# Cross-attention and mixture-of-experts kernel: new hand-written orders for all engines, no operation changed

## The chip, the cores and the metric

One core of one Trainium2 chip runs the kernel. The metric is device time in microseconds (us), from launch to the end. The profile comes from one such execution; its span is the time from the first to the last instruction on the core.

## What is computed

One transformer block on x of 4 x 256 x 256 (batch, position, width) in float32: a cross-attention with 16 heads of width 16 against a context of the same size, then a feed-forward part in which each position uses 2 of 8 experts. Cut to what matters:

```python
def attn(query, kv):                       # query = layernorm(x)
    Q, K, V = query @ Wq.T + bq, kv @ Wk.T + bk, kv @ Wv.T + bv
    a = softmax(einsum('bhsd,bhtd->bhst', Q, K) * 0.25)
    return einsum('bhst,bhtd->bhsd', a, V) @ Wo.T + bo
def ffn(x):                                # x = layernorm(x)
    scores = softmax(x @ G); w = scores kept for the 2 best experts, else 0
    out  = (silu(x @ gate) * (x @ up) * w) @ down
    return out + ((x @ lora_A) * w) @ lora_B
x = x + attn(layernorm(x), ctx)
x = x + ffn(layernorm(x))
```

## The kernel before, in words

Each of the four batches b is one tile of 256 positions. The whole program is cut into named stages, and every engine works through its own list of stages, written out by hand in `ORDERS`: "name:batch" or "name:batch.step", and for TensorE "@bank" with the PSUM bank that it writes (max and attn take that bank and the next). An engine runs its stages strictly in that order. Stages on different engines are tied by semaphores, so a stage whose input is late holds up all that is listed behind it on its engine. A TensorE stage also waits until the stage that last wrote its bank has been read out. SyncE issues nearly all transfers, also in its listed order.

The stages, in the order of the data, with the engine and the lines of the profile:

- st1, rs1, n1: layer norm of x. VectorE takes the moments (st1, L644 to L647), GpSimd makes 1/sqrt with a power (rs1, L431 to L437; shift at L437), ScalarE normalises (n1, L506; for batch 0 VectorE, L671). xT transposes it on TensorE (L857), xTE copies it out.
- k, v, q: the projections on TensorE (all products are at L813). khi, kw, qhi, qw (ScalarE, L525) and klo, qlo (VectorE L682 for batch 0, GpSimd L428) split k and q into two parts. vE (L532) copies v.
- kfill, qfill: memsets of the stacked tiles (GpSimd L393, VectorE L657, ScalarE L485); `ones` (L398) and `earlier` (L401, L402) are other constants on GpSimd. edge: two memsets of one column each on VectorE.
- ks0, ks1, qs0, qs1: SyncE copies the parts into the stacked tiles (L337, L344, L352, L359). Each ks and qs stage first waits for the fill of its tile. Batch 3 uses batch 0's tiles again. SyncE also issues wd, a weight of the last product (L302, L303).
- max (L886): scores, two heads at a time; mx (VectorE, L715): their row maxima. mrow (TensorE, L892) transposes the maxima once all eight mx of a batch are done, mrE (ScalarE, L538) copies them, ms (SyncE, L363) sends them into the stacked q.
- attn (L901): the scores again with the maximum taken off; e (ScalarE, L544): exponential; u (L911): times v. uT, rd (VectorE, L719, L725), um (GpSimd, L442), un (VectorE, L730): division by the sum. o: output product, after ah (ScalarE, L604) and al (VectorE, L778). x2 (VectorE, L734) adds it to x; xo (GpSimd, L448) has added the bias.
- st2, rs2, x2T (L933), x2hi, x2w, x2lo: the second layer norm's moments and transposes. low: gate logits and LoRA part, lowE copies it; r1, r2, ex, r3: weights of the experts. glu: gate and up products, in two steps; th (ScalarE, L582) and h (VectorE, L773, L775) their activation; wh (L318) and wl (L310) weigh them.
- hT, lT (L960, L965): transposes; hThi, lThi (ScalarE), hTlo (VectorE, L789) and lTlo (L793) split them; down: the last product, in two steps for batch 3; res (L802) adds, out stores.
- Weights: ws, wsl, wfc (L702), wlc, mean (L871), mlow take the mean out of the feed-forward weight; bw (VectorE, L688 to L692) and bias (L867), bp prepare the output bias. wkh, wkl, wvh, wvl, wfh, wfl, woh, wol, wdh, wdl split weights.

bw is a tensor_scalar and two additions. The wait at a stacked copy reads

```python
                if name == "qs0":
                    if b < NSTACK:
                        wait(sp, "qfill", b)
                    ...
                    wait(sp, "qhi", b)
                    for g in (0, 2):
                        sp.dma_start(part_rows(qstack[b], g), parts_of(q_hi[:, b % 2])).then_inc(q_stacked[b], 16)
```

Of the kernel before, what the change touches and what calls it, by code (L numbers as in the profile page):

```python
# [49 lines left out]

ORDERS = {
    "tensor": """
        k:0@6 xT:0@4 v:0@5 q:0@0 k:1@4 bias@5 xT:1@3 mean@0 v:1@2 max:0.4@0 max:0.3@6 xT:2@5 q:1@3 max:0.2@6
        max:0.0@4 max:0.1@0 v:2@2 k:2@3 max:0.5@0 max:0.7@6 max:0.6@4 q:2@2 max:1.0@0 max:1.1@6 xT:3@3 mrow:0@4
        k:3@5 max:1.2@2 max:1.3@6 q:3@4 max:1.4@2 attn:0.0@6 max:1.5@0 attn:0.1@2 max:1.6@6 attn:0.2@4 max:1.7@0
        attn:0.3@2 max:2.0@6 u:0.0@5 mrow:1@4 attn:0.4@0 max:2.1@2 attn:0.5@6 u:0.1@5 attn:0.6@0 max:2.2@2
        attn:0.7@6 u:0.2@5 attn:1.0@0 max:2.3@2 attn:1.1@6 u:0.3@5 attn:1.2@0 max:2.4@2 attn:1.3@6 u:1.0@5
        max:2.6@0 max:2.5@2 attn:1.4@6 o:0@4 attn:1.5@2 max:2.7@0 attn:1.6@6 u:1.1@5 max:3.1@2 max:3.0@0
        mrow:2@7 x2T:0@4 v:3@5 max:3.3@6 max:3.2@2 attn:1.7@0 mlow@4 u:1.2@5 attn:2.0@6 max:3.4@0 attn:2.1@2
        u:1.3@5 attn:2.3@0 attn:2.2@6 max:3.5@2 low:0@4 attn:2.5@0 attn:2.4@2 max:3.6@6 u:2.0@5 u:2.1@5  # L60
        attn:2.6@0 attn:2.7@2 max:3.7@6 glu:0.1@4 mrow:3@0 glu:0.0@7 o:1@6 attn:3.1@0 attn:3.3@2 attn:3.0@4
        u:2.2@7 u:2.3@7 attn:3.2@0 attn:3.4@4 attn:3.5@2 u:3.0@7 u:3.1@7 x2T:1@6 attn:3.6@4 attn:3.7@2 lT:0@1
# [6 lines left out]
        chi:3 qhi:1 qw:1 wfh n1:3 vE:2 khi:2 kw:2 qhi:2 xTE:3 mrE:0 qw:2 khi:3 kw:3 qhi:3 e:0.0 qw:3 e:0.1-3
        mrE:1 e:0.4-7 e:1.0-6 mrE:2 x2hi:0 x2w:0 vE:3 e:1.7 wdh e:2.0-1 e:2.3 e:2.2 woh e:2.5 e:2.4 lowE:0  # L70
        ah:1.1 e:2.6 ah:1.0 mrE:3 th:0.1 e:2.7 th:0.0 ex:0 ah:2.0 e:3.1 e:3.0 e:3.3 e:3.2 e:3.5 e:3.4 ah:2.1
        x2hi:1 x2w:1 e:3.6 lThi:0 e:3.7 ah:3.0 lowE:1 x2hi:2 hThi:0 ex:1 x2w:2 ah:3.1 th:1.0-1 lowE:2 ex:2
        x2hi:3 x2w:3 th:2.1 th:2.0 lowE:3 hThi:1 lThi:1 ex:3 th:3.1 th:3.0 hThi:2 lThi:2 lThi:3 hThi:3
    """,
    "vector": """
        warm edge kfill:2 kfill:0 st1:0 n1:0 st1:2 st1:1 klo:0 ws bw wsl qlo:0 st1:3 wfc mx:0.3-4 mx:0.2 mx:0.1
        mx:0.0 mx:0.5 mx:0.7 mx:0.6 mx:1.1 mx:1.0 mx:1.2-7 mx:2.0-1 uT:0.0 rd:0.0 mx:2.2 un:0.0 mx:2.3 uT:0.1
        rd:0.1 mx:2.4 un:0.1 mx:2.5-6 x2:0 mx:2.7 uT:1.0 mx:3.0-1 mx:3.3 mx:3.2 rd:1.0 mx:3.4 wlc uT:1.1 mx:3.5
        rd:1.1 st2:0 mx:3.6 un:1.1 un:1.0 uT:2.0 mx:3.7 al:1.0 rd:2.0 al:1.1 r1:0 un:2.0 h:0.1 h:0.0 r2:0 al:2.0
        x2:1 r3:0 uT:2.1 rd:2.1 st2:1 un:2.1 uT:3.0 al:2.1 rd:3.0 un:3.0 lTlo:0 x2:2 st2:2 r2:1 al:3.0 uT:3.1  # L80
# [944 lines left out]
```

## Time and profile before

| | us |
|---|---|
| median of 3 runs (109.81 to 111.5) | 110.0 |
| the profiled execution | 110.28 |
| its span | 108.5 |
| TensorE busy (matmuls) | 102.2 |
| VectorE busy | 92.0 |
| ScalarE busy | 76.7 |
| GpSimd busy | 55.4 |

Busy times add up what instructions of one engine take; the rest of the span the engine waits. Matmuls are pipelined and their ends are modelled, so a busy TensorE need not be at its peak. The granted TensorE clock is 1.0 of full speed over the whole span. A row of the timeline reads: start, length, engine, line, operation, what is written from what, number of instructions; in brackets the idle time ahead of it and who ended it.

### The profile page before, as it was taken

To read this page: it belongs to the slowest core of one execution; us is meant where nothing else is said; L and a number is where in the kernel's file an instruction comes from. 1 tells how busy PE (TensorE), PEld (TensorE's weight loads), DVE (VectorE), ACT (ScalarE), POOL (GpSimd) and SP (SyncE) were. 2 spreads that over 40 slices of the span, in tenths; PEclk is the share of its full clock that TensorE was granted. 3 is DMA by queue.
4 is the path that set the end of the run, shared out by engine and by line. 5 is a ranking of instruction groups with operands and counts; after the bars stand their busy time and mean duration, and the time that the engine had idled before them with its cause. 6 is when DMAs were issued, how large, how long until landed. Compare 5 with 4: busy or idle time off the path is not lost.

```text
span 108.5 us, 2396 instructions
## 1 busy us (share of the span) xinstructions
PE 102.2 (94%) x910; PEld 80.7 (74%) x910; DVE 92.0 (85%) x196; ACT 76.7 (71%) x140; POOL 55.4 (51%) x86
## 2 busy tenths in 40 slices
...
DMA packets 8469, 11.76 MB, mean 108 GB/s; under 512 B 713, under 2 KB 5002, under 8 KB 8458
## 3 DMA queue, kind: packets, MB, share of 16 engines
...
## 4 chain that ended last, share of the span: by engine, by line
PE 77%; DVE 6%; ACT 6%; POOL 6%; issue 2%; POOLq 0%
PE unit L813 40%; PE unit L911 12%; PE unit L901 9%; PE unit L886 8%; ACT probs L544 3%; DVE kstack L657 3%; PE unit L933 2%; POOL rstd L436 2%; PE unit L857 2%; PE unit L960 2%; POOL vaug L398 1%; DVE rowmax L715 1%; PE unit L892 1%; ACT xn L506 1%; PE unit L965 1%
## 5 line engine op out<-in xcount | busy, mean ns | idle before, releaser
L715 DVE TENSOR_REDUCE rowmax<-unit 128x4 f32<-128x1024 f32 x32 | 37.6, 1217 | 4.4 <-PE unit L886 4.3
L544 ACT ACTIVATE probs<-unit 128x1024 f32<-128x1024 f32 x32 | 31.2, 1027 | 2.7 <-PE unit L901 2.4
L911 PE MATMUL unit<-probs,vaug 128*32 128x256 f32 x256 | 16.3, 384 | 0.0
L901 PE MATMUL unit<-qstack,kstack 64*128 64x256 f32 x128 | 13.6, 310 | 1.1 <-DVE rowmax L715 0.7
L442 POOL TENSOR_TENSOR un<-uT,rden 128x256 f32<-128x256 f32 x8 | 5.0, 630 | 18.8 <-DVE rden L725 18.8
L901 PEld LDWEIGHTS unit<-qstack,kstack 64*128 64x128 f32 x128 | 9.1, 185 | 6.0 <-ACT probs L544 2.2
L886 PE MATMUL unit<-kstack,qstack 63*128 63x256 f32 x128 | 12.4, 296 | 0.6 <-ACT probs L544 0.6
L886 PEld LDWEIGHTS unit<-kstack,qstack 63*128 63x128 f32 x128 | 9.1, 185 | 3.5 <-issue 1.4
L911 PEld LDWEIGHTS unit<-probs,vaug 128*32 128x32 f32 x256 | 7.1, 109 | 5.1 <-ACT probs L544 0.2
L813 PE MATMUL unit<-xT,wq 128*128 128x256 f32 x32 | 7.8, 386 | 0.0
L813 PEld LDWEIGHTS unit<-xT,wq 128*128 128x128 f32 x32 | 5.8, 190 | 0.9
L719 DVE STREAM_TRANSPOSE uT<-unit 128x512 f32<-128x512 f32 x8 | 5.7, 710 | 0.8 <-PE unit L911 0.7
L463 POOL TENSOR_TENSOR x2T_lo<-x2T,x2T_hi 128x512 fp32r<-128x512 f32 x2 | 2.6, 1293 | 7.1 <-ACT x2T L563 7.1
L644 DVE BATCH_NORM_STATS2 stats<-xs 128x6 f32<-128x256 f32 x16 | 5.8, 403 | 0.0
L818 PE MATMUL unit<-warm 128*128 128x128 f32 x20 | 4.6, 429 | 1.1 <-DVE warm L655 1.1
L448 POOL TENSOR_TENSOR xs<-xs,bo_sb 128x256 f32<-128x256 f32 x8 | 5.6, 726 | 0.0
L525 ACT ACTIVATE q_hi<-unit,wq 128x256 fp32r<-128x256 f32 x8 | 3.3, 468 | 2.9 <-PE unit L813 2.9
L818 PEld LDWEIGHTS unit<-warm 128*128 128x128 f32 x20 | 4.3, 331 | 1.1 <-DVE warm L655 1.1
L428 POOL TENSOR_TENSOR q_lo<-q_whole,q_hi 128x512 fp32r<-128x512 f32 x3 | 3.9, 1290 | 2.1 <-ACT q_whole L525 2.1
L813 PE MATMUL unit<-wf,x2T 128*128 128x136 f32 x32 | 4.5, 283 | 0.0
L813 PEld LDWEIGHTS unit<-wf,x2T 128*128 128x128 f32 x32 | 4.1, 189 | 0.4 <-ACT x2T L563 0.2
L813 PE MATMUL unit<-cT,wk 128*128 128x256 f32 x16 | 4.3, 416 | 0.0
...
## 6 DMA issues: line engine op xcount, KB each, us to landing
kstack<-k_hi SPq DMA_DIRECT2D x8, 256.0 KB, 3.0
qstack<-q_hi SPq DMA_DIRECT2D x8, 256.0 KB, 2.6
xs<-x SPq DMA_DIRECT2D x4, 256.0 KB, 5.5
kstack<-k_lo SPq DMA_DIRECT2D x4, 256.0 KB, 3.3
qstack<-q_lo SPq DMA_DIRECT2D x4, 256.0 KB, 2.8
cT<-ctxT SPq DMA_DIRECT2D x3, 256.0 KB, 3.1
out<-xs SPq DMA_DIRECT2D x3, 256.0 KB, 2.5
...
```

The costliest lines, as they stand in the source:

```text
L428: pool.tensor_tensor(lo[:, b % 2], whole[:], hi[:, b % 2].bitcast(F32), ALU.subtract).then_inc(done[name], 1)
L442: pool.tensor_tensor(un[:, i].rearrange("p n h d -> p h n d"), uT[:, i, :, :, 0:HD], rden[:, i].unsqueeze(3).to_broadcast([P, 2, BLK, HD]) ...
L448: ins = pool.tensor_tensor(xs[:, b, t], xs[:, b, t], bo_sb[:], ALU.add)
L544: act.activation(probs[:, n % NPAIR], unit[BANK["attn", b, i] // 2][:], ACT.Exp, scale=SCALE)\
L644: ins = dve.bn_stats(stats[:, w, b, t], src[:, t])
L715: dve.tensor_reduce(rowmax[:, b % 2, :, :, i].rearrange("p t j -> p j t"), unit[BANK["max", b, i] // 2][:], AX.X, ALU.max).then_inc(done[" ...
L719: dve.transpose(uT[:, i].rearrange("p h n c -> p (h n c)"), work[BANK["u", b, 2 * i]].rearrange("p h s -> p (h s)")).then_inc(done["uT"], 1)
L813: ins = pe.matmul(dst, left(i, k), right(j, k), start=(n == 0), stop=(n == len(steps) - 1))
L818: pe.matmul(unit[3][:, 1, 0, 0:P], warm[:], warm[:], start=True, stop=True)
L886: ins = pe.matmul(pair[:, j, t], qstack[b][rows, i, t * P:(t + 1) * P], kstack[b][rows, i], start=True, stop=True)
L901: ins = pe.matmul(pair[:, j, t], kstack[b][rows, i, t * P:(t + 1) * P], qstack[b][rows, i], start=True, stop=True)
L911: ins = pe.matmul(dst[QUAD * j:QUAD * (j + 1), i % 2], vaug[:, b % NVALUE, t, 4 * i + j], probs[:, n % NPAIR, j % 2, t], start=(t == 0), s ...
```

## The change

All five lists of `ORDERS` are new; nothing else. Every stage stands in the lists as before and on the same engine, and every operation is as before; the waits follow from the lists. Two lines of the diff:

```diff
-        qfill:0 ident rs1:0 earlier ones rs1:2 rs1:1 rs1:3 wvl klo:1 clo:2 wkl qlo:1 clo:3 qfill:2 xo:2 klo:2
...
+        ident qfill:2 rs1:0 ones rs1:1 qfill:0 rs1:2 wvl klo:1 rs1:3 clo:2 wkl qlo:1 clo:3 xo:0 klo:2 qlo:2 xo:3
```

At the start of GpSimd's list, behind the ones of vaug and a first round of statistics (L431 to L437, which is batch 2 before and batch 1 now):

```order
 L436 TENSOR_TENSOR rstd<-vare,mhalf 128x2
 L437 TENSOR_TENSOR shift<-minus_mean,rstd 128x2
-L431 TENSOR_SCALAR vare<-mv 128x2
-L435 TENSOR_SCALAR minus_mean<-mv 128x2
-L436 TENSOR_TENSOR rstd<-vare,mhalf 128x2
-L437 TENSOR_TENSOR shift<-minus_mean,rstd 128x2
+L393 MEMSET qstack0 128x2048
 L431 TENSOR_SCALAR vare<-mv 128x2
 L435 TENSOR_SCALAR minus_mean<-mv 128x2
```

A round of statistics between the first and the next has gone back (batch 3's now comes behind wvl and klo:1), batch 1's and batch 2's have changed places, and the memset of qstack0, which stood first on GpSimd, has come in behind batch 1's. ScalarE's n1:1 and n1:2 and SyncE's x:1 and x:2 have changed places in the same way, wf is loaded ahead of x:2 and wo, and on TensorE bias has gone behind xT:1 and mean.

On TensorE, around the maxima of batch 0 (L892, mrow:0), before, from xT:3 (L857) and k:3 (the six pairs on cT and wk) to q:3 (L813 on xT and wq); kstack1 is batch 1:

```order
L886 MATMUL unit3<-kstack1,qstack1 128x256 x4
L857 MATMUL unit1<-ident,xn 128x128 x4
L892 MATMUL unit2<-ident,rowmax 16x128 x2
L813 MATMUL unit2<-cT_hi,wk_hi 128x256 x2
...
L886 MATMUL unit1<-kstack1,qstack1 128x256 x4
L886 MATMUL unit3<-kstack1,qstack1 128x256 x4
L813 MATMUL unit2<-xT,wq 128x256 x4
```

and now:

```order
L857 MATMUL unit1<-ident,xn 128x128 x4
L813 MATMUL unit2<-cT_hi,wk_hi 128x256 x2
...
L886 MATMUL unit1<-kstack1,qstack1 128x256 x4
L886 MATMUL unit3<-kstack1,qstack1 128x256 x4
L892 MATMUL unit2<-ident,rowmax 16x128 x2
L813 MATMUL unit0<-xT,wq 128x256 x4
```

mrow:0 has moved behind k:3 and two score pairs, directly ahead of q:3. On ScalarE mrE:0 now follows khi:3 and kw:3, and qw:3 comes ahead of e:0.0 instead of behind it; on SyncE ms:0 follows ks1:2, qs0:2 and ks0:2.

At the end of VectorE's list, before, from the last h (L773, L775) to the first res (L802):

```order
L773 SCALAR_TENSOR_TENSOR hid<-hid,unit 128x256
L775 TENSOR_TENSOR hid<-hid,unit 128x256
L318 TENSOR_TENSOR hid<-hid,weight_hid 128x256
L310 TENSOR_TENSOR low<-low,weight_low 128x128 x2
L793 TENSOR_TENSOR q_lo<-unit,q_hi 128x256
L318 TENSOR_TENSOR hid<-hid,weight_hid 128x256
L789 TENSOR_TENSOR k_lo<-unit,k_hi 128x512
L802 TENSOR_TENSOR xs<-unit,xs 128x512
```

and now:

```order
L773 SCALAR_TENSOR_TENSOR hid<-hid,unit 128x256
L775 TENSOR_TENSOR hid<-hid,unit 128x256
L310 TENSOR_TENSOR low<-low,weight_low 128x128 x2
L318 TENSOR_TENSOR hid<-hid,weight_hid 128x256 x2
L789 TENSOR_TENSOR k_lo<-unit,k_hi 128x512
L793 TENSOR_TENSOR q_lo<-unit,q_hi 128x256
L802 TENSOR_TENSOR xs<-unit,xs 128x512 x2
```

lTlo:2 (L793) and hTlo:2 (L789) have gone behind wl:3 (L310) and both wh:3 (L318). Further up, hTlo:0 has gone from ahead of un:3.1 to behind al:3.1, h:1.1 and r1:2, and lTlo:0 from ahead of x2:2 to ahead of rd:3.1. On TensorE lT:3 now writes bank 4, as hT:2 does, and comes behind hT:3.

For batch 3, SyncE's list was "qs1:3 ks1:3 qs0:3 ks0:3" and is "ks1:3 ks0:3 qs0:3 qs1:3 wd"; GpSimd's was "um:0.0 qlo:3 klo:3" and is "qlo:3 um:0.0 earlier klo:3". Where the feed-forward part of batch 0 begins, x2T:0 has gone behind v:3 on TensorE, and u:2.2 shares bank 5 with glu:0.1 now, where it was bank 7 with glu:0.0; VectorE's "h:0.1 h:0.0 r2:0" is "r2:0 h:0.0-1", and ScalarE's "e:2.7 th:0.0" is "wdh th:0.0".

## Rows read from the trace of the kernel before

**Rows 1.** Stretch, length, busy us of TensorE, weight loads, VectorE, ScalarE, GpSimd; clock.

```profile
84.67:101.20 16.53, 16.53 (x115) 15.04 (x114) 15.64 (x56) 8.12 (x25) 7.66 (x15) 1.00 0.01 1
```

**Rows 2.** Timeline of the start, 0 to 19 us.

```profile
0.78 1.81 POOL L393 MEMSET qstack<- 128x2048 f32 x1 [0.29 <-POOLq L1016]
...
10.17 0.72 POOL L436 TENSOR_TENSOR rstd<-vare,mhalf 128x2 f32<-128x2 f32 x1
...
11.44 0.35 DVE L688 TENSOR_SCALAR hid<-wo 128x256 f32<-128x256 f32 x1
...
11.61 1.09 ACT L506 ACTIVATE xn<-xs,shift,rstd 128x256 f32<-128x256 f32 x2 [0.29 <-POOL shift L437]
...
12.34 0.41 DVE L692 TENSOR_TENSOR hid<-hid,bo_row 1x256 f32<-1x256 f32 x1
...
12.35 1.19 POOL L436 TENSOR_TENSOR rstd<-vare,mhalf 128x2 f32<-128x2 f32 x1
...
13.99 0.59 PE L867 MATMUL unit<-hid,warm 128*128 128x256 f32 x2
...
14.99 0.66 PE L857 MATMUL unit<-ident,xn 128*128 128x128 f32 x4 [0.41 <-ACT xn L506]
...
18.16 0.74 PE L886 MATMUL unit<-kstack,qstack 63*128 63x256 f32 x8
```

**Rows 3.** Timeline of SyncE's issues, over the whole span.

```profile
13.50 1.18 SPq L352 DMA_DIRECT2D qstack<-q_hi  x2
...
14.72 0.61 SPq L359 DMA_DIRECT2D qstack<-q_lo  x1
...
30.15 0.64 SPq L363 DMA_DIRECT2D qstack<-mT  x1
...
46.23 2.71 SPq L352 DMA_DIRECT2D qstack<-q_hi  x2
...
48.98 1.26 SPq L337 DMA_DIRECT2D kstack<-k_hi  x2
```

**Rows 4.** Issues in narrow stretches (14.6 to 14.8, 49.55 to 49.7): size, us to landing.

```profile
qstack<-q_lo SPq DMA_DIRECT2D x1, 256.0 KB, 2.6
...
kstack<-k_hi SPq DMA_DIRECT2D x2, 256.0 KB, 3.1
```

**Rows 5.** Timeline around the first exponentials, 26 to 39 us.

```profile
31.75 0.84 ACT L525 ACTIVATE k_whole<-unit,wk 128x256 f32<-128x256 f32 x2
...
33.87 0.50 PE L901 MATMUL unit<-qstack,kstack 64*128 64x256 f32 x4
...
36.05 2.86 ACT L544 ACTIVATE probs<-unit 128x1024 f32<-128x1024 f32 x3
...
38.05 1.07 PE L911 MATMUL unit<-probs,vaug 128*32 128x256 f32 x16
```

**Rows 6.** Timeline of the passage to batch 3 and to the feed-forward part.

```profile
52.88 0.74 PE L886 MATMUL unit<-kstack,qstack 63*128 63x256 f32 x8 [0.63 <-ACT probs L544]
...
67.88 0.36 ACT L538 CAST mT<-unit 16x256 fp32r<-16x256 f32 x1 [0.95 <-PE unit L892]
...
70.36 0.42 DVE L775 TENSOR_TENSOR hid<-hid,unit 128x256 f32<-128x256 f32 x1
...
70.57 0.97 PE L901 MATMUL unit<-qstack,kstack 64*128 64x256 f32 x12
...
71.48 1.93 PE L911 MATMUL unit<-probs,vaug 128*32 128x256 f32 x32
```

**Rows 7.** Timeline of VectorE and TensorE towards the end.

```profile
83.94 0.69 DVE L789 TENSOR_TENSOR k_lo<-unit,k_hi 128x512 fp32r<-128x512 f32 x1
...
84.67 0.45 DVE L730 STREAM_TRANSPOSE attnT<-un 128x256 f32<-128x256 f32 x1
...
100.52 0.68 DVE L789 TENSOR_TENSOR k_lo<-unit,k_hi 128x512 fp32r<-128x512 f32 x1
...
101.35 0.47 PE L813 MATMUL unit<-cT_hi,k_hi 128*128 128x256 f32 x2
```

More of the change, by code:

```diff
@@ L52 @@
     "tensor": """
[L53 to L62, printed above, removed]
@@ L63 @@
-        o:2@7 low:1@0 u:3.2@5 u:3.3@5 x2T:2@6 hT:0@0 glu:1.0@2 glu:1.1@1 low:2@0 o:3@3 lT:1@7 glu:2.1@6 x2T:3@4
-        glu:2.0@3 low:3@5 hT:1@1 glu:3.0@2 lT:2@4 glu:3.1@0 down:0@5 hT:2@0 down:1@1 lT:3@6 hT:3@4 down:2@7
-        down:3.1@6 down:3.0@3
+        k:0@3 xT:0@1 v:0@4 q:0@5 k:1@0 xT:1@4 mean@1 bias@6 v:1@3 max:0.4@6 max:0.3@0 xT:2@5 q:1@3 max:0.2@6
+        max:0.0@4 max:0.1@0 v:2@2 k:2@3 max:0.5@0 max:0.7@6 max:0.6@4 q:2@2 max:1.0@0 max:1.1@6 xT:3@3 k:3@4
+        max:1.3@2 max:1.2@6 mrow:0@5 q:3@1 max:1.4@2 max:1.5@4 attn:0.0@6 attn:0.1@0 max:1.6@2 attn:0.2@4
@@ new lines @@
+        max:2.0@6 max:1.7@0 attn:0.3@2 u:0.0@4 mrow:1@5 attn:0.4@0 max:2.1@2 attn:0.5@6 u:0.1@4 attn:0.6@0
+        max:2.2@2 attn:0.7@6 u:0.2@5 attn:1.0@0 max:2.3@2 attn:1.1@6 u:0.3@5 attn:1.2@0 max:2.4@2 attn:1.3@6
+        u:1.0@5 max:2.6@0 max:2.5@2 attn:1.4@6 o:0@4 attn:1.5@2 max:2.7@0 attn:1.6@6 u:1.1@5 max:3.1@2 max:3.0@0
+        max:3.3@6 mrow:2@4 v:3@5 x2T:0@4 attn:1.7@0 max:3.2@2 u:1.2@5 mlow@4 attn:2.0@6 max:3.4@0 attn:2.1@2
+        u:1.3@5 attn:2.2@6 attn:2.3@0 max:3.5@2 low:0@4 max:3.6@6 attn:2.4@2 attn:2.5@0 u:2.0@5 u:2.1@5
@@ L66 @@
+        attn:2.7@2 max:3.7@6 attn:2.6@0 glu:0.1@5 mrow:3@2 glu:0.0@6 o:1@4 attn:3.1@0 attn:3.0@2 attn:3.2@6
+        u:2.2@5 u:2.3@5 attn:3.3@0 attn:3.4@2 u:3.0@6 u:3.1@6 attn:3.6@2 attn:3.7@4 x2T:1@0 o:2@1 attn:3.5@6
+        lT:0@2 low:1@3 x2T:2@0 u:3.2@4 u:3.3@4 hT:0@1 glu:1.1@6 low:2@2 glu:1.0@4 o:3@2 glu:2.0@5 x2T:3@6 lT:1@0
+        hT:1@2 glu:2.1@4 low:3@7 glu:3.0@1 lT:2@3 glu:3.1@2 down:0@7 hT:2@4 down:1@5 hT:3@6 lT:3@4 down:2@3
+        down:3.1@1 down:3.0@7
     """,
     "scalar": """
-        c:0 kfill:1 wq bo qfill:1 wkh khi:0 xTE:0 wvh vE:0 n1:2 qhi:0 n1:1 khi:1 xTE:1 kw:1 bp vE:1 chi:2 xTE:2
@@ L69 @@
[L69 to L73, printed above, removed]
+        c:0 qfill:1 wq bo kfill:1 wvh khi:0 xTE:0 vE:0 n1:1 qhi:0 khi:1 wkh kw:1 bp xTE:1 n1:2 vE:1 chi:2 chi:3
```

27 lines of the change are left out of this document (16 added, 11 removed).

## The prediction

> **What bounds the kernel now.** I read the table of stretches first. From 84.67 to 101.20 us TensorE is busy for all 16.53 us and VectorE for 15.64, at a granted clock of 1.00 [rows 1]; ahead of that TensorE stands only in a few short places. A new order removes no work, so it can win only stands of TensorE and the time before its first dense stretch, and it can lose wherever a stage is now reached before its input. So the second view was the timeline, one engine at a time: where does TensorE stand, and what ended the wait? There are four such places that the new orders touch, and one at the end where VectorE is as full as TensorE. I go through them in order of time. A lead won at one place is carried on only if each later place lets it through.
>
> **1. The start: -0.55 us.** Before, GpSimd works out batch 2's statistics ahead of batch 1's. Batch 2's are ready for ScalarE at 11.61; batch 1's follow, their power alone takes 1.19 us, and TensorE stands 0.41 us until 14.99 for xT:1, although it had started bias at 13.99 [rows 2]. In the new orders rs1:1 takes rs1:2's place and n1:1 takes n1:2's, so xn of batch 1 is ready 1.09 us after 11.61, at 12.70. TensorE is through k:1 at 13.99 and can transpose at once. From there xT:1, mean and v:1 take 18.16 - 14.99 = 3.17 us, and bias, now behind mean, at most 0.59 (its row; the ends of products are modelled, so the next can start earlier, and I put 0.45). That gives the first scores at 13.99 + 3.17 + 0.45 = 17.61 where they were at 18.16 [rows 2]. The new queue behind this: qfill:0, a memset of 1.81 us, stood first on GpSimd at 0.78 and now stands behind rs1:1; it would end at 11.61 + 1.81 = 13.42, while SyncE issued the stage that waits for it, qs0:0, at 13.50 [rows 2, 3]. That is 0.08 us of cover. The last part, qs1:0, is issued at 14.72 and lands 2.6 us later at 17.3 [rows 3, 4]. Both doors open by 17.6. Bounds: -0.6 if all hold; 0 if rs1:1 keeps its longer time (its power took 1.19 against 0.72 us for batch 2's, +0.47) and pushes qfill:0, qs0:0 and the landing. I take -0.55, since the row in the new place is batch 2's.
>
> **A rule weighed against this.** The long power of 12.35 ran beside a VectorE addition of 0.41 us that began at 12.34; 0.72 + 0.41 is 1.13, close to 1.19 [rows 2]. The Trainium skill (SBUF — State Buffer, section "Who interferes with whom") says that VectorE and GpSimd share one port pair as an exclusive lock, held for a whole instruction, taken by a VectorE operation with two SBUF inputs only against GpSimd work that reads, and by a VectorE tensor_scalar in a two-port mode against any. By that rule, the trace agrees for the power. By it the memset qfill:0, which reads nothing, could also hold up the tensor_scalar of bw; that is rival C.
>
> **2. First batch's maxima to the exponentials: +0.3 us.** mrow:0 ran between xT:3 and k:3. Now k:3 and two score pairs come first. The pieces between max:1.1 and q:3 are the same, so q:3 itself keeps the lead of 0.55, but mrow:0 comes a whole k stage and two score pairs later, and on ScalarE mrE:0 stands behind khi:3 and kw:3, which ended at 32.59 (31.75 + 0.84) before, 32.0 with the lead. mrE:0 adds 0.36 (the row of its fellow at 67.88), so ms:0 is issued at about 32.35 instead of 30.15, and its place on SyncE (now behind ks1:2, qs0:2 and ks0:2) is free by then, since their issues waited for parts that come earlier now [rows 3, 5, 6]. How long its 16 KB take is in no row; issue to the first attn that uses it was 30.15 to 33.87 with other work between, so the true value is below 3.7; the tightest bound is batch 3's: mrE:3 ends at 68.24 and attn:3.1 starts at 70.57, 2.3 [rows 5, 6]. With 2.3 attn:0.0 starts at 34.65 (before 33.87), e:0.0 after its 0.50 at 35.15. But qw:3, which stood between e:0.0 and e:0.1 and made ScalarE wait until 36.05, now comes ahead of e:0.0. Three exponentials took 2.86, so 0.95 each: e:0.2 ends at 35.15 + 2.86 = 38.0, and u:0.0, which needs its bank, starts where it did, 38.05 [rows 5]. That would eat the whole 0.55. If the 16 KB land by 34.0, ScalarE is ready for e:0.0 at 34.6 after qhi:3 and qw:3, and u:0.0 starts at 37.5: 0.1 of the lead lost. I take the middle, +0.3, bounds +0.1 and +0.55.
>
> **3. Batch 3's stacks: -0.3 us.** From u:0.0 to u:1.1 the order of TensorE is the same. Then it stands 0.63 us before max:3.1 at 52.88 [rows 6]. The row names an exponential, but e:1.5 had long been done; SyncE shows the real one: the last two ks0:3 transfers are issued from 48.98, the second at about 49.6, and land 3.1 later, at 52.7 [rows 3, 4]. They were late because the two issues of qs0:3 took 2.71 us where the pair at 13.50 took 1.18. New order: on GpSimd qlo:3, a subtraction like klo:3, leaves the place ahead of klo:3 and the small `earlier` takes it, so ks1:3 goes out some 0.6 us sooner (an estimate: 128x512 against 128x64 elements); but all six transfers, not five, now follow it. Issues at 0.6 each without the hold end near 48.6 and land by 51.2 to 51.7: the 0.63 us go. With the same hold they land at about 52.7: nothing goes. -0.3, bounds -0.63 and 0.
>
> **4. The switch to the feed-forward part: +0.1 us.** x2T:0 goes behind v:3, and the steps around h:0.0 and h:0.1 change places. u:2.2 shares a bank with one half of glu:0 and waits for the h that frees it; the second h ended at 70.78 (70.36 + 0.42), and TensorE reached u:2.2 at 71.48, so 0.70 us of cover [rows 6]. Before, h:0.1 was done while th:0.0 still ran; now h:0.0 comes first and h:0.1 behind it, so both follow th:0.0, the later of the two. That is two operations of 0.42 more behind it: 70.78 + 0.84 = 71.62, 0.14 past 71.48, with the lead on both sides. (On ScalarE wdh stands ahead of th:0.0 where e:2.7 did; I count them as equal. r2:0 goes ahead of both h, into the time in which VectorE waits for th:0.0.) +0.1, bounds 0 and +0.6 (the lead is lost on ScalarE).
>
> **5. The end: +0.7 us.** Here VectorE binds. Before, un:3.1 at 84.67 is followed nearly without a gap until hTlo:2 ends at 101.20 (15.64 of 16.53 us busy), and down:2 starts at 101.35 [rows 1, 7]. While GpSimd worked on um:3.1, VectorE did hTlo:0, 0.69 us at 83.94. Now nothing fills that wait: lTlo:0 goes ahead of rd:3.1, un:3.1 follows rd:3.1 directly, and hTlo:0 comes later. Between un:3.1 and the last part that down:2 needs, VectorE has the same operations plus hTlo:0. Besides, hTlo:2 now stands behind wl:3 and both wh:3, and lT:3 has hT:2's bank and waits for it. So down:2 is 0.69 us later against un:3.1; down:3 and the stores follow it. Bounds 0 (TensorE late by itself) and +0.7.
>
> **Sum.** -0.55 + 0.3 - 0.3 + 0.1 + 0.7 = +0.25 us. The profiled execution took 110.28 us, 0.28 above the median of the runs, 110.0. Against the median: 110.25, so 110.3. All bounds at their best: -0.6 + 0.1 - 0.63 = -1.1, 108.9; at their worst 0 + 0.55 + 0 + 0.6 + 0.7 = +1.85, 111.9. That the two small memsets stand second on VectorE is nothing new: they did before.
>
> **Rivals.** A, faster: the tail costs nothing, because VectorE takes hTlo:0's 0.69 us out of the 16.53 - 15.64 = 0.89 us in which it is idle there [rows 1], and the hold of SyncE is gone. For it: the idle time. Against: 56 instructions share it, so most of it is the short gap between one and the next that uses it. That is the best case, 108.9 (own range 108.6 to 109.5). B, slower: the long hold at the queue, 2.71 - 1.18 = 1.5 us, comes twice, on both pairs of the six transfers: last landing 51.5 + 3.0 = 54.5, 1.8 after the 52.7 of before, TensorE stands 1.7 more, the 0.3 of term 3 is not won, and 110.3 + 0.3 + 1.7 = 112.3. It decides once the last landing is over 52.9. For it: the hold has come once with five transfers; against: the pairs at 13.50 and 48.98 took 1.18 and 1.26 [rows 3]. C, slower by the port: the tensor_scalar of bw (0.35 us at 11.44 [rows 2]) comes to about 11.8 now, inside qfill:0, and waits to 13.42; bw, 1.31 in all (11.44 to 12.34 + 0.41), ends at 14.7, and qlo:0 with two operations of about 0.45 follows it: its part goes out at about 15.6, not 14.72, and lands at 18.2. The first scores come at about 18.25, and term 1 turns from -0.55 to +0.1: 110.95. For it: the tensor_scalar row; against: nothing in the trace shows a memset of GpSimd holding anything.
>
> **Chances.** The forecast 0.60, A 0.22, B 0.10, C 0.08. The range 108.6 to 111.9 holds the forecast with its bounds, A and C, and leaves B out. Two per cent of 110.0, about what a measurement of this kernel can tell from no change, are 107.8 and 112.2: slower by over 2% is B with a little less than C's tail, 0.10; faster needs more than all my bounds give, 0.04; within, 0.86.
>
> **What would show it.** Right: xT:1 at 14.0 with no stand, the first max near 17.6, mrow:0 behind max:1.2, u:0.0 between 37.5 and 38.05, no gap between hTlo:0's new place and lTlo:2, down:2 near 101.8. Wrong: a first max after 18.2 (term 1, C), TensorE waiting at max:3.1 over 0.6 us (3, B), u:2.2 behind h:0.1 by over 0.3 (4), or down:2 starting the moment TensorE is free (5, A). A new stand of TensorE over 0.5 us anywhere else would mean that I missed a wait.

## The result, and the profile after

| | before | after |
|---|---|---|
| median of the runs in one comparison (us) | 109.91 (109.79 to 111.5) | 110.87 (110.83 to 110.9) |
| ratio, 95% interval | | 1.0091 (1.0071 to 1.0111) |
| the profiled execution | 110.28 | 110.84 |
| its span | 108.5 | 109.0 |

The new orders make the kernel 0.9% slower: 1.0 us in the medians, 0.56 between the two profiled executions (that of before lies 0.37 above its median). Medians here are over all executions, while a ratio leaves out those in which the chip ran in a slower state, as in the 111.5. 110.87 lies inside the predicted range, 0.6 above the predicted 110.3, and the change is within the predicted 2%.

Where the time went is seen best when the span is cut at starts of TensorE stages that stand in the same place in both orders. Each column is the time from one start to the next, in us, read from the traces.

| kernel | to first max | to v:2 | to q:3 | to u:0.1 | to u:1.1 | to max:3.1 | to hT:0 | to down:2 | to the end |
|---|---|---|---|---|---|---|---|---|---|
| before | 18.16 | 3.89 | 9.52 | 8.71 | 10.89 | 1.70 | 29.75 | 18.71 | 7.11 |
| after | 17.85 | 4.14 | 9.64 | 9.08 | 10.88 | 1.42 | 29.72 | 19.00 | 7.29 |
| difference | -0.31 | +0.25 | +0.12 | +0.37 | -0.01 | -0.28 | -0.03 | +0.29 | +0.18 |

The sum of the differences is +0.6. Two stretches win, and five lose. Now the rows of after that answer to those of before, from its timeline: start, duration, engine, line, operation, in brackets the idle time ahead and what ended it.

```profile
11.49 2.05 DVE L688 TENSOR_SCALAR hid<-wo 128x256 f32<-128x256 f32 x1
11.58 1.80 POOL L393 MEMSET qstack<- 128x2048 f32 x1
13.91 0.60 PE L857 MATMUL unit<-ident,xn 128*128 128x128 f32 x4
15.32 0.53 SPq L359 DMA_DIRECT2D qstack<-q_lo  x1
17.85 0.74 PE L886 MATMUL unit<-kstack,qstack 63*128 63x256 f32 x8 [0.32 <-DMA qstack<-q_lo]
19.65 1.14 ACT L497 CAST cT_hi<-cT 128x512 fp32r<-128x512 f32 x2 [1.25 <-DMA cT<-ctxT]
20.69 0.58 ACT L513 COPY xT<-unit 128x512 f32<-128x512 f32 x1
...
32.66 0.64 SPq L363 DMA_DIRECT2D qstack<-mT  x1
34.79 0.90 PE L901 MATMUL unit<-qstack,kstack 64*128 64x256 f32 x8 [0.59 <-DMA qstack<-mT]
37.32 0.50 PE L886 MATMUL unit<-kstack,qstack 63*128 63x256 f32 x4 [0.17 <-ACT probs L544]
37.87 3.69 DVE L715 TENSOR_REDUCE rowmax<-unit 128x4 f32<-128x1024 f32 x3 [0.38 <-PE unit L886]
38.24 1.07 PE L911 MATMUL unit<-probs,vaug 128*32 128x256 f32 x16 [0.17 <-ACT probs L544]
...
45.93 1.26 SPq L337 DMA_DIRECT2D kstack<-k_hi  x2
47.23 1.94 SPq L352 DMA_DIRECT2D qstack<-q_hi  x2
49.21 0.61 SPq L359 DMA_DIRECT2D qstack<-q_lo  x1
53.01 0.98 PE L886 MATMUL unit<-kstack,qstack 63*128 63x256 f32 x12 [0.35 <-DMA qstack<-q_lo]
...
84.90 0.45 DVE L730 STREAM_TRANSPOSE attnT<-un 128x256 f32<-128x256 f32 x1 [0.74 <-POOL un L442]
87.72 0.68 DVE L789 TENSOR_TENSOR k_lo<-unit,k_hi 128x512 fp32r<-128x512 f32 x1
100.67 0.68 DVE L789 TENSOR_TENSOR k_lo<-unit,k_hi 128x512 fp32r<-128x512 f32 x1
101.27 0.41 DVE L793 TENSOR_TENSOR q_lo<-unit,q_hi 128x256 fp32r<-128x256 f32 x1
101.73 0.51 PE L813 MATMUL unit<-cT_hi,k_hi 128*128 128x256 f32 x2
```

**Start.** xT:1 starts at 13.91 without a stand, where it stood until 14.99 [rows 2]. But the tensor_scalar of bw, 0.35 us before [rows 2], takes 2.05 beside the memset qfill:0, and the last part of the first stack, qs1:0, goes out at 15.32 instead of 14.72 [rows 3]; TensorE, free at 17.53, stands 0.32 for it. Then ScalarE waits 1.25 us for context transfers that SyncE issued behind qs1:0, xTE:2 stands behind those casts, max:0.0 needs its bank, and at v:2 the lead is 0.07.

**Middle.** ms:0 goes out at 32.66 (30.15 [rows 3]) and attn:0.0 stands 0.59 for it until 34.79 (33.87 [rows 5]). max:1.7 runs at 37.32, behind max:2.0, and VectorE, which takes mx:1.7 first, stands 0.38 until 37.87. u:0.0 starts at 38.24, not 38.05 [rows 5].

**Batch 3 and the end.** The pair of qs0:3 takes 1.94 (2.71 [rows 3]), and the stand ahead of max:3.1 is 0.35 (0.63 [rows 6]). At the end VectorE stands 0.74 ahead of un:3.1, in the place where hTlo:0 was [rows 7]; hTlo:0 comes at 87.72, hTlo:2 ends at 101.35, lTlo:2 at 101.68, and down:2 starts at 101.73 (101.35 [rows 7]).

### The profile page after: what moved, and what is told of

The parts are those of the page before. It is cut to its first block, busy times and chain, and to the rows that moved or that the text cites. A ratio compares the mean times of both kernels' runs of the same rounds, so it can differ in the third digit from the quotient of the medians.

```text
span 109.0 us, 2402 instructions
## 1 busy us (share of the span) xinstructions
PE 102.6 (94%) x910; PEld 80.7 (74%) x910; DVE 92.9 (85%) x196; ACT 76.0 (70%) x140; POOL 55.1 (51%) x86
## 3 DMA queue, kind: packets, MB, share of 16 engines
HBM read 4.21 MB, written 1.05 MB: 48 GB/s over the span
## 4 chain that ended last, share of the span: by engine, by line
PE 65%; DVE 12%; DMA 7%; ACT 4%; SPq 3%; POOL 3%; issue 2%
PE unit L813 35%; PE unit L911 11%; PE unit L901 6%; PE unit L886 6%; DMA qstack<-q_lo 6%; DVE kstack L657 3%; ACT probs L544 3%; PE unit L933 2%; DMA qstack<-mT 2%; DVE hid L688 2%; DVE stats L644 2%; SPq L352 2%; PE unit L960 2%; POOL k_lo L428 1%; SPq L337 1%
## 5 line engine op out<-in xcount | busy, mean ns | idle before, releaser
L813 PE MATMUL unit<-xT,wq 128*128 128x256 f32 x32 | 7.7, 383 | 0.0
L813 PEld LDWEIGHTS unit<-xT,wq 128*128 128x128 f32 x32 | 5.8, 190 | 0.8
L318 POOL TENSOR_TENSOR hid<-hid,weight_hid 128x256 f32<-128x256 f32 x6 | 3.6, 614 | 3.9 <-DVE hid L775 3.0
L525 ACT ACTIVATE k_hi<-unit,wk 128x256 fp32r<-128x256 f32 x8 | 3.4, 470 | 2.5 <-PE unit L813 2.5
L582 ACT ACTIVATE hid<-unit,half_rstd 128x256 f32<-128x256 f32 x8 | 3.7, 472 | 1.9 <-PE unit L813 1.9
L730 DVE STREAM_TRANSPOSE attnT<-un 128x256 f32<-128x256 f32 x8 | 3.4, 428 | 1.5 <-POOL un L442 1.5
```

The source lines that it names most:

```text
L813: ins = pe.matmul(dst, left(i, k), right(j, k), start=(n == 0), stop=(n == len(steps) - 1))
```

## Experiments

All kernels are the kernel before or the kernel after with rows of the lists moved. Times are medians; the ratio is to the kernel before in the same comparison. Where lists have fewer lines, line numbers in a profile are a few lower. First, the stretches of all kernels, from their traces, with the time of their profiled execution:

| kernel | to first max | to v:2 | to q:3 | to u:0.1 | to max:3.1 (from u:1.1) | to down:2 (from hT:0) | to the end | profiled execution |
|---|---|---|---|---|---|---|---|---|
| before | 18.16 | 3.89 | 9.52 | 8.71 | 1.70 | 18.71 | 7.11 | 110.28 |
| before, again | 18.18 | 3.90 | 9.52 | 8.72 | 1.48 | 18.70 | 7.12 | 110.04 |
| after | 17.85 | 4.14 | 9.64 | 9.08 | 1.42 | 19.00 | 7.29 | 110.84 |
| after, again | 17.79 | 4.19 | 9.66 | 9.08 | 1.49 | 19.02 | 7.30 | 110.88 |
| e1 qfill:0 first | 17.52 | 3.92 | 9.62 | (10.09) | 1.39 | 19.03 | 7.28 | 111.25 |
| e2 mrow back | 17.86 | 4.12 | 9.58 | 9.06 | 1.79 | 19.06 | 7.30 | 111.11 |
| e3 xTE:2 first | 17.46 | 3.96 | 9.62 | 9.08 | 1.41 | 19.03 | 7.28 | 110.18 |
| e4 tail back | 17.85 | 4.11 | 9.64 | 9.08 | 1.44 | 18.82 | 7.13 | 110.50 |
| e5 = e1 + e4 | 17.52 | 4.40 | 9.64 | 9.08 | 1.42 | 18.82 | 7.13 | 110.37 |
| e7 middle back | 17.86 | 4.17 | 9.58 | 8.71 | 1.68 | 19.02 | 7.29 | 110.73 |
| e10 VectorE's tail | 17.86 | 4.10 | 9.64 | 9.08 | 1.46 | 18.78 | 7.28 | 110.65 |
| e9 = e1, e3, e7, e4 | 17.46 | 3.97 | 9.51 | 8.71 | 1.18 | 18.81 | 7.13 | 109.14 |
| e6 before, batch 1 first | 17.55 | 3.89 | 9.52 | 8.71 | 1.85 | 18.69 | 7.16 | 109.80 |
| e8 = e6, ks first | 17.56 | 3.90 | 9.55 | 8.71 | 1.05 | 18.69 | 7.16 | 109.02 |

Two stretches are not shown because they are the same in all: u:0.1 to u:1.1 (10.88 to 10.90) and max:3.1 to hT:0 (29.72 to 29.78). In the profiled execution of e1 the granted clock was 0.50 from about 37.0 to 40.4 us, so only its rows ahead of that and its stretches further on are read.

### Do the profiles repeat?

> The kernel before, profiled once more, to see which of its rows repeat. Theory 'hold by chance': the 2.71 us that SyncE took for the pair of qs0:3 at 46.23 are not part of the program; this time the pair takes 1.2 to 2.0, max:3.1 starts by 52.5 instead of 52.88 and the profiled execution takes about 109.9, like the median of the runs. Rival 'hold belongs to the order': the pair takes 2.7 again, max:3.1 stands 0.6 us again, and the execution takes 110.3 again.

> The kernel after, once more, beside the other kernels of this comparison. Theory 'tail and exponentials': over the kernel before it is 0.4 late at u:1.1 and 0.5 more between hT:0 and the end, 110.9 if before takes 110.0 to 110.1. Rival 'one bad profile': a loss of 0.9 belongs to the first comparison alone and it comes out within 0.3 of before.

Before, again: 110.15, ratio 1.0008 (0.9959 to 1.0057). The pair of qs0:3 took 2.56 (2.71 in the first profile): the hold is no chance of one execution, and the first theory falls. Only the stand behind it is shorter, 0.41. After, again: 110.9 beside 110.09, ratio 1.0079 (1.0062 to 1.0097). Its stretches agree with those of the first profile within 0.07: the loss is real, and of two places as expected, 0.36 to 0.37 on the way to u:0.1 and 0.5 from hT:0. One stretch does not repeat: to max:3.1 it took 1.70 and 1.48 in before, 1.42 and 1.49 in after. In the second pair of profiles nothing is won there (+0.01), and the two executions lie 0.84 apart (110.88 and 110.04), near the difference of the medians, where the first pair had 0.56. The -0.28 of the first table is that one execution of before.

### The tensor_scalar beside the memset

```diff
-        ident qfill:2 rs1:0 ones rs1:1 qfill:0 rs1:2
+        qfill:0 ident qfill:2 rs1:0 ones rs1:1 rs1:2
```

> The kernel after, with the memset qfill:0 back as GpSimd's first stage. Theory 'port': the tensor_scalar of bw took 2.05 us only because the memset of 1.80 us ran beside it; now it takes 0.35, bw ends near 12.8, qlo:0 starts at 13.5, qs1:0 is issued at 14.75 instead of 15.32 and lands near 17.2, and the first max starts at 17.5 to 17.6 with no stand (17.85 with 0.32 before it). c:3 and c:2 go out 0.6 earlier as well, so the time falls by 0.2 to 0.4, to 110.5 to 110.7. Rival 'input': the tensor_scalar waited for the transfer of wo, and takes 2.05 us or starts after 13 as before; first max at 17.85, time 110.9.

Timeline of e1, the same three instructions:

```profile
11.49 0.32 DVE L688 TENSOR_SCALAR hid<-wo 128x256 f32<-128x256 f32 x1
...
14.79 0.61 SPq L359 DMA_DIRECT2D qstack<-q_lo  x1
...
17.52 0.74 PE L886 MATMUL unit<-kstack,qstack 63*128 63x256 f32 x8
```

0.32 instead of 2.05, at the same start: the 1.7 us were the memset's. The transfer of wo is excluded, since the instruction starts at 11.49 in both. The first max has no stand and starts at 17.52. The time is 110.5, ratio 1.0051 (1.0008 to 1.0093), so some 0.3 to 0.4 of the loss belongs to this one row, at the edge of what the comparisons tell apart (e4 and e5 below differ by this row in one comparison, and there it is 0.25).

```diff
-        vE:1 chi:2 chi:3 xTE:2 qhi:1
+        vE:1 xTE:2 chi:2 chi:3 qhi:1
```

> The kernel after, with xTE:2 ahead of chi:2 and chi:3 on ScalarE (one row moved). Theory 'bank': max:0.0 stood because its bank waited for xTE:2, which stood behind the two casts that waited 1.25 us for context transfers. Now xTE:2 runs at 19.2, max:0.0 starts at 20.5 and ends the three by 21.7, v:2 starts at 21.7 instead of 21.99, and the lead of 0.3 of the first max is kept to q:3 (31.35 instead of 31.63): 110.5 to 110.7. Rival 'inputs of v and k': the casts and the subtractions behind them come 0.6 later, v:2 or k:2 waits for them, and nothing is won or 0.2 lost: 110.9 to 111.1.

110.69, ratio 1.0051 (1.001 to 1.0092). max:0.0 starts at 20.78, v:2 at 21.42 and q:3 at 31.04, near what the theory has. But part of that is not this edit's. In this profile the memset came 0.56 us earlier by itself, and the timeline gives a second dose of the first question:

```profile
11.02 1.80 POOL L392 MEMSET qstack<- 128x2048 f32 x1
11.71 1.26 DVE L687 TENSOR_SCALAR hid<-wo 128x256 f32<-128x256 f32 x1
```

The memset ends at 12.82, the tensor_scalar at 12.97; in after they end at 13.38 and 13.54. Long overlap, shorter overlap, none: 2.05, 1.26, 0.32; and wherever the two run side by side, the tensor_scalar ends 0.15 to 0.16 behind the memset. What the edit of e3 itself is worth depends on when the context lands. Without it, the stretch to v:2 takes 3.92 in e1 but 4.40 in e5 (below), where the second context transfer landed at 19.56 instead of 19.08, the casts end at 20.72 and xTE:2 at 21.20. With it, 3.96 here and 3.97 in e9. So it was worth nothing in one execution and 0.4 in another, and the medians (110.69 here, 110.5 in e1) show no gain.

### mrow, or the order of the scores

```diff
-        ... xT:3@3 k:3@4 max:1.3@2 max:1.2@6 mrow:0@5 q:3@1 ...
+        ... xT:3@3 mrow:0@5 k:3@4 max:1.3@2 max:1.2@6 q:3@1 ...
-        ... xTE:3 khi:3 kw:3 mrE:0 qhi:3 qw:3 e:0.0-3 ...
+        ... xTE:3 mrE:0 khi:3 kw:3 qhi:3 qw:3 e:0.0-3 ...
-        ... ks1:2 qs0:2 ks0:2 ms:0 qs1:2 ...
+        ... ks1:2 ms:0 qs0:2 ks0:2 qs1:2 ...
```

> The kernel after, with mrow:0 on TensorE, mrE:0 on ScalarE and ms:0 on SyncE back ahead of the k stage of batch 3, as in the kernel before. Theory 'landing': u:0.0 and u:0.1 were late by 0.2 and 0.4 because the 16 KB of ms:0 landed late; now ms:0 is issued near 30.3, attn:0.0 starts at about 33.9 instead of 34.79, e:0.0 at 35.1, right after qw:3, and u:0.0 at 38.0 instead of 38.24: time 110.5 to 110.7. Rival 'maxima': VectorE's row of maxima, without a gap from 25.6 to 41, sets u:0.1, and nothing is won: 110.9.

110.91, ratio 1.0071 (1.003 to 1.0112). attn:0.0 starts at 34.06 and u:0.0 at 38.07, but the stretch to u:0.1 is 9.06, as in after (9.08). The rival's outcome came, nothing is won: the late landing of ms:0, on which the prediction built its second term, is by itself not the cause of the loss at u:0.1. The timeline of e2 shows what comes instead:

```profile
35.22 0.50 PE L899 MATMUL unit<-qstack,kstack 64*128 64x256 f32 x4 [0.76 <-ACT q_whole L523]
...
37.01 0.74 PE L884 MATMUL unit<-kstack,qstack 63*128 63x256 f32 x8
37.78 3.61 DVE L713 TENSOR_REDUCE rowmax<-unit 128x4 f32<-128x1024 f32 x3 [0.27 <-PE unit L884]
```

attn:0.1 takes the bank of q:3 and waits for qw:3; and max:1.7 still comes behind max:2.0 (the pair at 37.01), while VectorE takes mx:1.7 first and stands 0.27. So the next kernel moves the whole piece back:

```diff
-        ... k:3@4 max:1.3@2 max:1.2@6 mrow:0@5 q:3@1 max:1.4@2 max:1.5@4 attn:0.0@6 attn:0.1@0 max:1.6@2 attn:0.2@4
-        max:2.0@6 max:1.7@0 attn:0.3@2 u:0.0@4 ...
+        ... mrow:0@5 k:3@4 max:1.3@2 max:1.2@6 q:3@5 max:1.4@2 attn:0.0@6 max:1.5@0 attn:0.1@2 max:1.6@6 attn:0.2@4
+        max:1.7@0 attn:0.3@2 max:2.0@6 u:0.0@4 ...
-        ... xTE:3 khi:3 kw:3 mrE:0 qhi:3 qw:3 e:0.0-3 ...
+        ... xTE:3 mrE:0 khi:3 kw:3 qhi:3 e:0.0 qw:3 e:0.1-3 ...
-        ... ks1:2 qs0:2 ks0:2 ms:0 qs1:2 ...
+        ... ks1:2 ms:0 qs0:2 ks0:2 qs1:2 ...
```

> The kernel after, with the stretch from k:3 to u:0.0 as before: mrow:0, mrE:0 and ms:0 early, attn and max of the first batch taking turns one by one, q:3 no longer in a bank that attn:0.1 takes, and qw:3 behind e:0.0. Theory 'interleaving': what is lost between q:3 and u:0.1 (9.08 us in after, 8.71 in before) is the order of the scores, of which mrow alone was a part; the stretch falls back to 8.7, u:0.1 starts at 40.3 instead of 40.7, and the time is 110.4 to 110.6. Rival 'banks and inputs further on': the stretch stays at 9.0 or the gain is lost again before max:3.1 (52.9 to 53.0), and the time is 110.9.

110.56, ratio 1.0046 (1.0016 to 1.0076). The stretch is 8.71 to the hundredth, in this kernel and in e6, e8 and e9. u:0.1 starts at 40.32. The whole loss of 0.37 comes back with this piece: mrow:0, and the order of the scores against the banks and VectorE's maxima. mrow:0 alone does not bring it (e2); the order of the scores without mrow:0 was not run. Which of the swaps does it was not taken apart by a run, but the traces point at max:2.0 ahead of max:1.7. attn:0.5 takes the bank of max:2.0, and VectorE is done with mx:2.0 at 39.80 in before and 39.83 in e7, at 40.22 in after and 40.14 in e2, where it stood 0.38 and 0.27 for max:1.7. attn:0.5 starts at 39.95 and 39.98, 40.28 and 40.20, and u:0.1 follows 0.34 to 0.43 later. Timeline of before, VectorE's five maxima without a stand between them, and attn:0.5:

```profile
34.05 5.75 DVE L715 TENSOR_REDUCE rowmax<-unit 128x4 f32<-128x1024 f32 x5 [0.23 <-PE unit L886]
...
39.95 0.41 PE L901 MATMUL unit<-qstack,kstack 64*128 64x256 f32 x4
```

and attn:0.5 in after:

```profile
40.28 0.50 PE L901 MATMUL unit<-qstack,kstack 64*128 64x256 f32 x4
```

Part of the gain is gone at max:3.1 (1.68 instead of 1.42), where the pair of qs0:3 was held 2.66 us; the section on the hardware comes back to that.

### The end

```diff
-TensorE  hT:0 glu:1.1 low:2 glu:1.0 o:3 glu:2.0 x2T:3 lT:1 hT:1 ...
+TensorE  hT:0 glu:1.0 glu:1.1 low:2 o:3 lT:1 glu:2.1 x2T:3 glu:2.0 ...
-VectorE  lTlo:0 rd:3.1 un:3.1 r3:1 al:3.1 h:1.1 r1:2 hTlo:0 h:1.0 ...
+VectorE  lTlo:0 rd:3.1 hTlo:0 un:3.1 r3:1 al:3.1 h:1.0-1 r1:2 ...
...
```

The last rows of ScalarE, GpSimd and SyncE go back likewise.

> The kernel after, with every engine's order from hT:0 on as in the kernel before (on TensorE from hT:0, on VectorE from lTlo:0, on ScalarE from x2w:2, GpSimd's and SyncE's last rows), and after's order ahead of it. Theory 'tail': the stretch from hT:0 to the end took 26.3 us in after and in each of its variants, 25.8 in before; it falls back to 25.8, and the time falls by 0.5 to about 110.4. Rival 'carried in': the stretch is long because GpSimd's um:3.1 and the first half of the feed-forward part come in another state; it stays at 26.2 or more and the time at 110.9.

110.49, ratio 1.0044 (1.0024 to 1.0064), 0.4 below after. From hT:0 to the end it takes 18.82 + 7.13 = 25.95, against 26.29 in after and 25.82 in before: the rows of the end cost 0.34 of the 0.47, and 0.13 stays. The rival can hold for this 0.13 at most, since what comes into the stretch is the same as in after.

```diff
-VectorE  rd:3.1 un:3.1 r3:1 al:3.1 h:1.1 r1:2 hTlo:0 h:1.0
+VectorE  rd:3.1 hTlo:0 un:3.1 r3:1 al:3.1 h:1.1 r1:2 h:1.0
-ScalarE  ex:1 ah:3.1 th:1.1 lowE:2 hThi:0 th:1.0
+ScalarE  ex:1 hThi:0 ah:3.1 th:1.1 lowE:2 th:1.0
-TensorE  hT:3@6 lT:3@4
+TensorE  hT:3@6 lT:3@0
```

> The kernel after with only those rows of the end moved back that the prediction named: hTlo:0 on VectorE ahead of un:3.1 (and hThi:0 on ScalarE ahead of ah:3.1, which it needs), and lT:3 in a bank of its own instead of hT:2's. TensorE's order stays. Theory 'VectorE binds': this alone gives back what the end lost, hT:0 to the end falls from 26.3 to 25.9, 110.5. Rival 'TensorE's own order': the stretch is longer because x2T:3 and lT:1 now come before the second half of glu:2 and x2T:3 waits for x2:3; it stays at 26.2 or more, 110.8.

110.6, ratio 1.0068 (1.0039 to 1.0098). With only hTlo:0 (and the hThi:0 that it reads) and lT:3's bank moved, hT:0 to down:2 falls from 19.00 to 18.78. Timeline of e10:

```profile
84.12 0.65 DVE L789 TENSOR_TENSOR k_lo<-unit,k_hi 128x512 fp32r<-128x512 f32 x1
84.94 0.45 DVE L730 STREAM_TRANSPOSE attnT<-un 128x256 f32<-128x256 f32 x1 [0.17 <-POOL un L442]
...
101.08 0.41 DVE L793 TENSOR_TENSOR q_lo<-unit,q_hi 128x256 fp32r<-128x256 f32 x1
101.55 0.50 PE L813 MATMUL unit<-cT_hi,k_hi 128*128 128x256 f32 x2
```

hTlo:0 fills the wait for um:3.1, un:3.1 starts where it did, and down:2 comes 0.18 sooner though TensorE's order stayed. So VectorE binds there, as predicted; for TensorE's own order 0.07 is left (18.78 against 18.71). lT:3's bank, moved as well, did not end the wait: in after and in e10 down:2 starts 0.05 to 0.06 behind the end of lTlo:2. The last stretch stays at 7.28 (7.13 with the whole end back): the rest of the end's order costs 0.15 more behind down:2, and which of its rows does it was not taken apart.

Both edits, qfill:0 first and the end back, in one kernel:

> The two edits together: qfill:0 first on GpSimd, and the order from hT:0 on as before. Theory: the first max at 17.5 and the stretch from hT:0 at 25.8 add up, -0.35 and -0.5, to 110.0, level with before. Rival: the start's gain is lost at attn:0.0, which waits for mT, and only the tail's stays: 110.4.

110.24, ratio 1.0019 (0.9999 to 1.004). The end's gain is there, the start's only in part: the first max is at 17.52 but v:2 at 21.92, since the context landed late for the casts ahead of xTE:2 in this execution (the stretch took 3.92 in e1 and 4.40 here, from the same rows up to that point). The rival named the wrong place, attn:0.0, for the right kind of loss.

### One part of the change alone, and the sum of the repairs

```diff
-VectorE  n1:0 st1:2 st1:1           GpSimd  ones rs1:2 rs1:1 rs1:3
+VectorE  n1:0 st1:1 st1:2           GpSimd  ones rs1:1 rs1:2 rs1:3
-ScalarE  vE:0 n1:2 qhi:0 n1:1       SyncE   wk wv x:2 x:1 wo
+ScalarE  vE:0 n1:1 qhi:0 n1:2       SyncE   wk wv x:1 x:2 wo
```

> The kernel before with one part of the change alone: batch 1 ahead of batch 2 in st1 on VectorE, rs1 on GpSimd, n1 on ScalarE and x on SyncE; nothing else moves, qfill:0 stays first. Theory: xT:1 starts near 14.5 behind bias with no stand, the first max at 17.6 to 17.7 instead of 18.16, and since mrow:0 and everything behind it keep the order of before, u:0.0 starts 0.4 to 0.5 sooner and the time is 109.5 to 109.7. Rival 'chain of maxima': VectorE's maxima from mx:0.0 to mx:2.0 take the lead away, u:0.1 starts at 40.3 as before, and the time is that of before.

109.58 beside 110.09, ratio 0.9939 (0.9906 to 0.9972): faster than before and after, if by less than 2%. The first max is at 17.55, and the stretches behind it are those of before to 0.01, so the whole 0.6 arrives at u:1.1 (50.56 against 51.18); the rival, a chain of maxima that eats the lead, falls. Then it meets batch 3's stacks:

```profile
45.60 2.93 SPq L352 DMA_DIRECT2D qstack<-q_hi  x2
48.58 1.26 SPq L337 DMA_DIRECT2D kstack<-k_hi  x2
...
52.41 0.73 PE L886 MATMUL unit<-kstack,qstack 63*128 63x256 f32 x8 [0.78 <-ACT probs L544]
```

The pair of qs0:3 is held 2.93, and TensorE stands 0.78. Next, with the change's order of these stacks as well:

```diff
-GpSimd  um:0.0 qlo:3 klo:3 um:0.1        SyncE  ms:1 qs1:3 ks1:3 qs0:3 ks0:3
+GpSimd  qlo:3 um:0.0 klo:3 um:0.1        SyncE  ms:1 ks1:3 ks0:3 qs0:3 qs1:3
```

> The best kernel so far (before with batch 1 ahead of batch 2) with one more part of the change: qlo:3 ahead of um:0.0 on GpSimd, and ks1:3, ks0:3, qs0:3, qs1:3 as SyncE's order for batch 3. Theory 'k first': from u:1.1 to max:3.1 it takes 1.4 us as in after, not 1.85 as in the best kernel, since klo:3 is 0.6 earlier; the time falls by 0.3 to 0.4 to 109.2. Rival 'same hold': one pair of the six transfers is held up 0.7 to 2 us whatever their order, the last still lands near 52.2, and the time stays at 109.6.

```profile
43.86 0.54 SPq L344 DMA_DIRECT2D kstack<-k_lo  x1
44.45 1.24 SPq L337 DMA_DIRECT2D kstack<-k_hi  x2
45.73 1.26 SPq L352 DMA_DIRECT2D qstack<-q_hi  x2
47.04 1.36 SPq L359 DMA_DIRECT2D qstack<-q_lo  x1
...
51.65 0.74 PE L886 MATMUL unit<-kstack,qstack 63*128 63x256 f32 x8
```

109.0 beside 110.06, ratio 0.9938 (0.9907 to 0.9969). No pair is held, only the last single transfer (1.36); it goes out by 48.40 instead of 49.84, and max:3.1 starts at 51.65 without a stand. Against e6 the medians say 0.6 us more, the ratios say nothing more, and the two were not in one comparison; the profiled executions (109.80 and 109.02) and the stretch to max:3.1 (1.85 and 1.05) speak for a gain.

Last, after with the edits of e1, e3, e7 and e4 together:

> The kernel after with all repairs at once: qfill:0 first, xTE:2 ahead of the context casts, the stretch from k:3 to u:0.0 and the one from hT:0 on as before. What is left of the change is batch 1 ahead of batch 2, the order of batch 3's stacks and the order between u:0.0 and hT:0. Theory: the repairs add up, -0.35 to -0.55 at the start, -0.4 in the middle, -0.35 at the end, to 109.7, as fast as the kernel before with batch 1 first. Rival: the parts that are left cost something themselves, and it stays above 110.

109.62, ratio 0.9981 (0.9952 to 1.001). The repairs add up as expected, 1.3 below after by the medians and 1.1 by the ratios (two comparisons), and the median is that of e6. The profiled execution is its fastest (109.14); beside e8 its stretches differ by more than 0.1 only at max:3.1 (0.13) and ahead of down:2 (0.12), but the medians by 0.6. What its other executions lose is in no profile and stays open.

## Why the prediction was right, and where its sum was wrong

The class and the range held, the predicted value was 0.6 too low, and the sum of +0.25 was made of terms that were wrong in both directions. That the total came out near is in part luck. About half of the 0.6 is the base: the rows came from an execution of 110.28, on which +0.25 gives 110.53, and 110.84 came; I put the sum on the median, 110.0, but after has no such difference between its profiled execution and its median (110.84, 110.87). Against the measured stretches:

**Term 1, -0.55; measured -0.31 at the first max, -0.07 at v:2.** The step that failed is one that the term took without saying it: that bw still takes the time of its row. That qfill:0 would end at 13.42 and that qs0:0 had 0.08 us of cover was right (13.38; issued at 13.56). But the row of 0.35 was taken beside other work than now. The mechanism is rival C's, to which I gave 0.08: it named the instruction, the memset and the stage that is late. Its price was too high by 0.4 (first scores at 18.25; 17.85 came): it put bw's end at 14.7 (14.50 came), qs1:0 at 15.6 (15.32) and its landing 2.6 behind that (2.4); the first of these is too late because it counted the whole tensor_scalar again behind the memset. C's total, 110.95, is nearer to the 110.87 than mine is, but by other losses than it counted. The second half of this loss was in no term: that the casts of the context, behind a transfer issued after qs1:0, stood ahead of xTE:2, whose bank max:0.0 needs. I had followed the lead up to the first max and then wrote that "q:3 itself keeps the lead of 0.55" without reading the next three banks. At q:3 nothing is left (31.63, 31.58 before): the 0.12 lost between v:2 and q:3 is in no term either, and its cause stays open.

By the rule that I weighed there, of the Trainium skill (SBUF — State Buffer, section "Who interferes with whom"), a GpSimd instruction holds the shared port pair for its whole length against a tensor_scalar in a two-port mode. With that rule the trace agrees on the length: 2.05 and 1.26 us until 0.15 to 0.16 behind the memset's end, 0.32 without it. On who comes first it does not: the same section of the Trainium skill gives the pair to whoever issues first, but in after the tensor_scalar's row starts at 11.49, ahead of the memset's at 11.58, and still it ends behind it.

**Term 2, +0.3; measured +0.37 from q:3 to u:0.1, +0.13 to u:0.0.** The size is right by accident. attn:0.0 could start 2.1 us after the issue of ms:0 (I had 2.3) and was late nearly as I had worked out (34.79, with hardly a lead; I had 34.65 with one of 0.55), but e2 takes that lateness away and wins 0.1 at u:0.0 and nothing at u:0.1. (The lower bound of +0.1 does not follow from its own figures: u:0.0 at 37.5 is the whole lead of 0.55 kept.) What the step left out is the order of the scores themselves. I treated the pairs of max and attn as equal pieces; e7 brings the whole 0.37 back with their order against the banks and against VectorE's maxima, mrow:0 included.

**Term 3, -0.3; measured -0.28 in the first pair of profiles, +0.01 in the second.** So no gain is shown, and the agreement in size is luck: the 0.63 that the term starts from was 0.41 when before was profiled again. klo:3 was 0.36 sooner (43.98, 44.34 before), where I had 0.6. The hold that I thought might go stayed, at one pair and smaller; in e8, where it falls on the last single transfer, the full 0.63 goes.

**Term 4, +0.1; measured 0 (-0.03).** u:2.2 started at 71.53 (71.48 before); its h had ended at 71.47. The chain came as I had it, only shorter: h ended 0.69 later than before, where I had counted 0.84, and the 0.70 us of cover were used up to the last 0.06. The stretch from max:3.1 to hT:0 is the same in every kernel.

**Term 5, +0.7; measured +0.29 to down:2 and +0.18 behind it.** The step holds: VectorE stands 0.74 where hTlo:0 was, and e10, which fills that wait again, gives 0.22 of the 0.29 back. Mis-sized is "the same operations plus hTlo:0", which I priced at its full 0.69. The stretch of VectorE from un:3.1 to the last split that down:2 needs, lTlo:2, in after (its length, VectorE's busy time, instructions, clock):

```profile
84.90:101.68 16.78, 15.95 (x57) 1.00 0.00 0
```

16.78 us against 16.53 [rows 1]: +0.25. The idle time in it is 0.83, as before 0.89, so rival A's point, that the idle time swallows hTlo:0, falls; its other half, a queue without the hold, did not come either. The busy time grew by 0.31 only: the subtraction into diff (L749), 0.59 us in the old place (88.97 in before, beside GpSimd), took 0.32 in the new one, and 0.08 of res:0 now lies behind. Besides un:3.1 itself came 0.23 later (84.90, 84.67 before), 0.14 of it behind hT:0, and down:2 now starts 0.05 behind the last split where it was 0.15. The 0.18 behind down:2 was in no term.

**Signs named ahead.** xT:1 at 14.0 (13.91), mrow:0 behind max:1.2 (31.41) and down:2 near 101.8 (101.73) came as written, the last by a different sum. First max near 17.6 and u:0.0 by 38.05 did not (17.85, 38.24). u:2.2 was not late by 0.3, and VectorE has no gap between hTlo:0's new place and lTlo:2, as named. The one new stand of TensorE over 0.5 us, 0.59 ahead of attn:0.0, is the landing that term 2 counted. Rival B, the hold twice, did not come: one hold, last landing at 52.9.
